# A nine-matmul group of one image of a pair, moved on TensorE from ahead of the mixing to behind the short groups of the second feature

## The chip, the cores and the metric

The kernel runs on one core of one Trainium2 chip. The metric is device time in microseconds (us). A core has a matmul engine (TensorE, PE in the rows, with its weight loads as PEld), a vector engine (VectorE, DVE), an activation engine (ScalarE, ACT), GpSimd (POOL) and a queue that issues transfers (SyncE, SPq). Each engine runs its own instructions in the order written; between engines only semaphores set an order. SBUF is the memory that the engines read, PSUM the one that TensorE writes its sums to.

## The reference, cut to what matters

The input is x of 16 images, 32 channels, 32 by 32 pixels. The first block is dense: each convolution sees x and all the features before it.

```
x1 = relu(conv2d(x, w1, b1, 2, 2))                      # 3x3, padding 2, dilation 2
x2 = relu(conv2d(concat(x, x1), w2, b2, 2, 2))
x3 = relu(conv2d(concat(x, x1, x2), w3, b3, 2, 2))
x4 = relu(conv2d(concat(x, x1, x2, x3), w4, b4, 2, 2))
fea = relu(concat(x, x1, x2, x3, x4))                   # 160 channels
fea = einsum('ij,bcjk,lk->bcil', H, fea, H)             # a 32-point transform on rows and columns
out = conv2d(fea, w6, b6, 1, 1) + x
```

The second block takes `out` through three convolutions with inputs and weights rounded to 4 bits (1x1 to 192 planes, 3x3 by plane, 1x1 back to 32) and adds its input. The change doesn't touch it.

## The kernel before

Images go through the dense block in eight pairs. `step(s, ...)` works on pair s; u is 0 or 1, the image in the pair. There are nine steps: 0, 1 and 2 are written out, 3 to 6 run in a loop of two bodies, 7 and 8 are written out. Step s computes the features of pair s (the convolutions) and, in between, mixes and transforms the pair before, p = s - 1. Step 8 only finishes pair 7.

**Convolutions.** A feature is held in `D[f][u]` as four shifted copies of 32 channels on 128 partitions, in a high and a low half of the float32 value, so that one product takes three matmuls (high by high, high by low, low by high). With three column shifts a full group is 9 matmuls of 128x512 (`conv`, L654 to L662). The 128 output rows of a group hold two features' sums at once. On x itself (f = 0) there are two groups per image: the first (weights 0) gives features 1 and 2 and goes to bank 0 of `conv_ps[u]`, the second (weights 1) gives features 3 and 4 and opens bank 1. Both stand in `conv0` (L682). On feature 1 there are the short groups, six matmuls (`conv1_alone`, L706, with L698 into `conv_ps` and L702 into `mix_ps`), and a full group into bank 1 (`conv1`, L712). On feature 2 there is one full group (`conv2`, L716), on feature 3 again short groups (`conv3`, L721).

**From a sum to the next feature.** ACT takes the sum from PSUM (`relu` L287 and L278, `take_part` L295), DVE adds the parts (`add_parts`, L417 and L419) and splits the feature into its halves (`split`, L406 and L408), the queue copies the shifted partitions (`halos`, L205 and L207), and PE waits for these copies on `halo_in`.

**Mixing.** `mix(p, u)` (L752) makes eight products of three matmuls from `F_hl` (L745) and one from `X4` (L749) in the four banks of `mix_ps`; ACT takes each to `Y` (`take_mix`, L330). `stage1` (L770) transforms one direction out of `Y`, again into `mix_ps`, at the end of a step. DVE turns that result into `Zt` (`turn_s1`, L450), once for each image, and it does so in the step after, right behind the split of feature 1 of image 0. `stage3` (L779) transforms the other direction, DVE turns it back (L457) and adds it up (L473).

**What sets the order around the change.** The order is written by hand for each engine. In a step PE runs `conv0` of both images, `mix(p, 0)`, `conv1_alone` of both, `conv1` of both, `stage3` of both, `conv2` of both, `mix(p, 1)`, `conv3` of both, `stage1`. `mix_ready` (L725) makes the mixing wait on `f_lo` and on `zt_done`: since `mix(p, 0)` overwrites the banks that `stage1` wrote, both transposes L450 of the step must have ended first. `zt_done` starts at GRANT, so in steps 0 and 1 nothing waits on it; in step 1 PE waits for `scales_ready` instead, behind `spread_weights` (L675), which DVE gives in L524 after the split of image 1. ACT holds a loop-like order too: at the end of a step `high_4` and `copy_4` of both images (L313, L320), and then `relu(s, 1, 0)` of the next step. The group that the change moves signals `x_used[1]`, on which ACT's `high_x` of the next pair waits.

Of the kernel before, what the change touches and what calls it, by code (L numbers as in the profile page):

```python
# [70 lines left out]
def dense_block(nc, x_res, x_pads, x_mix, w_conv, bias, w_mix, h_cols, h_rows, b6, w_int, ident_in, keep):  # L71
# [7 lines left out]
    with ExitStack() as ctx:  # L79
# [88 lines left out]
        def is_first(s):  # L168
            return isinstance(s, int) and s == 0

        def has_finish(s):

            return not (isinstance(s, int) and s < 2)

        def is_second(s):
            return isinstance(s, int) and s == 1

        def is_last(s):
            return isinstance(s, int) and s == PAIRS
# [470 lines left out]
        def _(pe):  # L650
# [3 lines left out]
            def conv(u, f, n, bank, start):  # L654

                for d in range(3):
                    for h, (wp, xp) in enumerate(((0, 0), (0, 1), (1, 0))):
                        last = nc.tensor.matmul(conv_ps[u][:, bank, :], w_hl[:, wp, n, d, :],  # L658
                                                D[f][u][:, xp, :, 2 * d:2 * d + S],
                                                start=start and d == 0 and h == 0,  # L660
                                                stop=d == 2 and h == 2, skip_group_check=True)
                return last  # L662

            def weights(s, n):
                if is_first(s):
                    pe.wait_ge(w_ready, n)
# [11 lines left out]
            def transform_ready():  # L678
                pe.wait_ge(h_in, 32)
                pe.wait_ge(w_ready, NM + 2)  # L680

            def conv0(s, u):  # L682
                pe.wait_ge(x_split[u], s + 1)
                if not is_first(s):
                    pe.wait_ge(added[u], s * 2)
                weights(s, 1)
                conv(u, 0, 0, 0, True).then_inc(conv_done[u], 1)
                weights(s, 2)
                conv(u, 0, 1, 1, True).then_inc(x_used[u], 1)

            def conv_alone(s, u, f, n):

                weights(s, n + 1)
                bank, side = conv_ps[u][:, (f - 1) // 2, :], side_sums(u, f)
                for d in range(3):
                    last = nc.tensor.matmul(bank, w_hl[:, 0, n, d, :], D[f - 1][u][:, 1, :, 2 * d:2 * d + S],  # L698
                                            start=False, stop=d == 2, skip_group_check=True)
                last.then_inc(conv_done[u], 1)  # L700
                for d in range(3):
                    last = nc.tensor.matmul(side, w_hl[:, 1, n, d, :], D[f - 1][u][:, 0, :, 2 * d:2 * d + S],  # L702
                                            start=d == 0, stop=d == 2, skip_group_check=True)
                last.then_inc(conv_done[u], 1)

            def conv1_alone(s, u):  # L706
                pe.wait_ge(halo_in[1][u], (s + 1) * 32)
                if not is_first(s):
                    pe.wait_ge(y_out, (s - 1) * 16 + (5 + u))
                conv_alone(s, u, 2, 2)  # L710

            def conv1(s, u):  # L712
                weights(s, 4)
                conv(u, 1, 3, 1, False)
# [10 lines left out]
            def mix_ready(p, u):  # L725

                pe.wait_ge(f_lo[u], p + 1)
                if banks(p, u) is not sums_ps:
                    for done in (zt_done, st_done) if u else (zt_done,):
                        pe.wait_ge(done, p * 2 + GRANT)  # L730

            def mix_x4_ready(p, u):
                pe.wait_ge(x4_lo[u], p + 1)
                pe.wait_ge(x4_copied[u], p + 1)

            def mix_rows(p, u, g):

                h, k = g // 4, slice(NP * (g % 4), NP * (g % 4) + NP)
                if g >= 4:
                    pe.wait_ge(y_out, (p * 2 + u) * 8 + (g - 3))  # L740
                elif banks(p, u) is sums_ps and g % 2 == 0:
                    pe.wait_ge(added[g // 2], 2 * PAIRS)
                y = banks(p, u)[:, g % 4, 0:MIX]
                for n, (wp, xp) in enumerate(((0, 0), (0, 1), (1, 0))):
                    nc.tensor.matmul(y, F_hl[u][:, xp, h, k], mix_hl[:, wp],  # L745
                                     start=n == 0, stop=False, skip_group_check=True)

            def mix_x4(p, u, g):
                nc.tensor.matmul(banks(p, u)[:, g % 4, 0:MIX], X4[u][:, g // 4, NP * (g % 4):NP * (g % 4) + NP],  # L749
                                 mix4_hl[:], start=False, stop=True, skip_group_check=True).then_inc(y_done, 1)  # L750
# [8 lines left out]
            def stage1(p, *us):  # L759

                pe.wait_ge(y_out, p * 16 + 8 * (us[-1] + 1))
                pe.sem_inc(s1_begun, 1)
                out = banks(p, us[0])
                for d in range(3):
                    for j in range(4):
                        k = slice(32 * j, 32 * j + 32)
                        for dy in range(3):
                            at = 96 * d + 32 * dy
                            y = Y[k, us[0]:us[-1] + 1, :, at:at + 32].rearrange("k u g o -> k (u g) o")
                            last = nc.tensor.matmul(out[32 * dy:32 * dy + 32, j, 0:PX // 4 * len(us)], hc[k, d], y,  # L770
                                                    start=d == 0, stop=d == 2, skip_group_check=True)
                last.then_inc(s1_done, 1)

            def stage3(p, u):

                pe.wait_ge(zt_done, p * 2 + (u + 1 + GRANT))
                zt = Zt[:, u, :].rearrange("p (o q l) -> p q o l", q=4, o=C)
                for q in range(4):
                    last = nc.tensor.matmul(banks(p, u)[32 * q:32 * q + 32, 2 + u, 0:PX // 4], hr[:], zt[:, q],  # L779
                                            start=True, stop=True, skip_group_check=True)  # L780
                last.then_inc(s3_done, 1)

            def step(s, odd, batch):
                p = s - 1
                dct = not is_first(s)
                if is_last(s):
                    mix_ready(p, 0)
                    for g in range(4):
                        mix_rows(p, 0, g)
                    mix_x4_ready(p, 0)  # L790
                    for g in range(4):
                        mix_x4(p, 0, g)
                    for g in range(4, 8):
                        mix_rows(p, 0, g)
                        mix_x4(p, 0, g)
                    pe.wait_ge(zt_done, p * 2 + GRANT)
                    for u in range(2):
                        stage3(p - 1, u)
                    mix_ready(p, 1)
                    for g in range(4):  # L800
                        mix_rows(p, 1, g)
                    mix_x4_ready(p, 1)
                    for g in range(4):
                        mix_x4(p, 1, g)
                    stage1(p, 0)
                    for g in range(4, 8):
                        mix_rows(p, 1, g)
                        mix_x4(p, 1, g)
                    stage3(p, 0)
                    stage1(p, 1)  # L810
                    stage3(p, 1)
                    return
                conv0(s, 0)
                conv0(s, 1)
                if is_second(s):
                    transform_ready()
                    spread_weights()
                    pe.wait_ge(scales_ready, 1)
                if dct:
                    mix(p, 0)  # L820
                conv1_alone(s, 0)
                conv1_alone(s, 1)
                conv1(s, 0)
                conv1(s, 1)
                if has_finish(s):
                    pe.wait_ge(y_out, p * 16 + 8)
                    stage3(p - 1, 0)
                    stage3(p - 1, 1)
                conv2(s, 0)
                conv2(s, 1)  # L830
                if is_first(s):
                    turn_peaks()
                if dct:
                    mix(p, 1)
                conv3(s, 0)
                conv3(s, 1)
                if dct:
                    stage1(p, 0, 1)

            steps(pe, step)  # L840


# [481 lines left out]
```

## Time and profile before

| | us |
|---|---|
| median of 3 runs | 429.36 |
| lowest, highest | 428.33, 430.48 |
| the profiled execution's own time | 426.66 |
| span of the profiled execution, first to last instruction | 424.9 |
| PE busy | 371.5 (87% of the span) |
| DVE busy | 299.0 (70%) |
| ACT busy | 232.0 (55%) |
| mean granted clock of TensorE | 0.956 of full speed |

In rows of the timeline the columns are start in us, duration in us, engine, line, operation, output<-inputs, shape and type, the count of instructions merged in the row, and in brackets the idle time before it with what ended that time. Matmuls overlap in the pipeline, so that a row's end lies a little behind the start of the next. The dense block ends at 328 us of the span; the quantised block takes the rest.

### The profile page before, as it was taken

How to read it: one execution, taken by the hardware profiler on the slowest of the kernel's cores; microseconds unless marked ns; L12 is line 12 of the kernel's file. 1: busy time of each engine (PE TensorE's matmuls, PEld its weight loads, DVE VectorE, ACT ScalarE, POOL GpSimd, SP SyncE). 2: the span in 40 equal slices, each digit the busy share in tenths (PEclk: the TensorE clock that was granted, in tenths of full speed). 3: DMA queues.
4: the chain of work that ended last, by engine and by line, in shares of the span. 5: the costliest groups of instructions: out<-in, count | busy, mean ns of one | idle time of the engine just before them, and what ended most of it. 6: DMA issues, size and time to landing. Idle time of an engine off the chain costs nothing. (4 is left out here: it accounts for less than half of the span.)

```text
span 424.9 us, 7855 instructions
## 1 busy us (share of the span) xinstructions
PE 371.5 (87%) x2772; PEld 262.9 (62%) x2772; DVE 299.0 (70%) x552; ACT 232.0 (55%) x378; POOL 18.1 (4%) x18
## 2 busy tenths in 40 slices
PE   4785898999999999999999999999984573799596
PEld 3563686677868778786877878687662221455332
DVE  5546635965884796588479568845976899577866
ACT  5133643655575375457537546752755695177640
POOL 3000000000000000000000000000001700022000
PEclk9998899999999999999999999999998599699969
DMA  7555124532423353242335324034200000000004
GB/s 246 124 146 155 46 53 101 141 76 66 117 77 80 91 151 84 63 108 80 79 92 147 86 64 107 23 77 105 68 3 0 2 0 0 0 4 2 2 26 173
DMA packets 19533, 32.56 MB, mean 77 GB/s; under 512 B 4528, under 2 KB 11568, under 8 KB 19504
## 3 DMA queue, kind: packets, MB, share of 16 engines
q1 hardware_dynamic: 19504, 32.17, 28.9%
q8 instruction: 18, 0.29, 0.3%
q14 instruction: 11, 0.09, 0.1%
HBM read 11.38 MB, written 2.10 MB: 32 GB/s over the span
## 5 line engine op out<-in xcount | busy, mean ns | idle before, releaser
L658 PE MATMUL sums_ps<-D,w_hl 128*128 128x512 f32 x576 | 148.1, 414 | 14.1 <-DVE D L424 6.0
L658 PEld LDWEIGHTS sums_ps<-D,w_hl 128*128 128x128 f32 x576 | 109.8, 193 | 53.5 <-DMA D<-D 8.7
L330 ACT ACTIVATE Y<-mix_ps 128x288 f32<-128x288 f32 x120 | 49.0, 411 | 32.9 <-PE mix_ps L749 20.9
L745 PE MATMUL mix_ps<-mix_hl,F_hl 128*128 128x288 f32 x360 | 65.1, 298 | 1.5 <-DVE St L457 0.7
L745 PEld LDWEIGHTS mix_ps<-mix_hl,F_hl 128*128 128x128 f32 x360 | 55.0, 190 | 5.0 <-issue 2.6
L287 ACT ACTIVATE r<-sums_ps,bias_sb 64x512 f32<-64x512 f32 x32 | 21.9, 683 | 66.2 <-PE sums_ps L658 66.1
L417 DVE TENSOR_TENSOR r<-mix_ps,r 64x512 f32<-64x512 f32 x16 | 11.1, 694 | 43.5 <-PE mix_ps L702 22.0
L406 DVE CAST D<-r 64x512 fp32r<-64x512 f32 x48 | 19.8, 412 | 25.5 <-ACT r L287 25.5
L1151 PE MATMUL ps<-q_q,q_diag 64*64 64x512 bf16 x576 | 34.7, 400 | 2.0 <-DVE q_q L1043 2.0
L955 ACT ACTIVATE q_I<-ps,w_bias 128x1024 f32 x24 | 25.4, 1111 | 18.9 <-PE ps L1151 18.9
L749 PE MATMUL mix_ps<-mix_hl,X 96*128 96x288 f32 x120 | 35.3, 298 | 0.0
L408 DVE TENSOR_TENSOR D<-r,D 64x512 fp32r<-64x512 f32 x48 | 32.9, 685 | 1.7
L698 PE MATMUL sums_ps<-D,w_hl 128*128 128x512 f32 x96 | 29.7, 420 | 4.1 <-DMA D<-D 4.1
L1151 PEld LDWEIGHTS ps<-q_q,q_diag 64*64 64x64 bf16 x576 | 19.3, 108 | 17.0 <-issue 3.8
L295 ACT ACTIVATE r<-sums_ps,bias_sb 64x512 f32<-64x512 f32 x32 | 21.1, 682 | 14.4 <-PE sums_ps L698 14.2
L440 DVE SCALAR_TENSOR_TENSOR X<-r,X 32x512 fp32r<-32x512 f32 x32 | 21.8, 681 | 8.1 <-ACT X L313 7.6
L313 ACT ACTIVATE X<-r 32x512 fp32r<-32x512 f32 x32 | 20.2, 630 | 12.9 <-DVE r L419 12.5
L1130 PE MATMUL ps<-q_xq,w_q 128*128 128x386 bf16 x72 | 17.1, 372 | 9.1 <-DVE q_xq L1008 5.2
L770 PE MATMUL mix_ps<-Y,hc 32*32 32x512 f32 (+1 forms) x576 | 24.3, 567 | 0.0
L698 PEld LDWEIGHTS sums_ps<-D,w_hl 128*128 128x128 f32 x96 | 17.4, 193 | 9.1 <-DMA D<-D 5.9
L473 DVE SCALAR_TENSOR_TENSOR values<-St,b_sb,xb 64x128 f32<-64x128 f32 (+1 forms) x64 | 22.2, 346 | 0.9
L431 DVE SCALAR_TENSOR_TENSOR F_hl<-F,F_hl 128x1024 fp32r<-128x1024 f32 x16 | 19.5, 1224 | 4.4 <-ACT F_hl L304 3.7
(121 smaller groups left out, 437.6 us busy)
## 6 DMA issues: line engine op xcount, KB each, us to landing
D<-D SPq DMA_DIRECT2D x96, 126.0 KB, 2.4
F<-r SPq DMA_DIRECT2D x96, 64.0 KB, 2.0
x_own<-in_x_pads SPq DMA_DIRECT2D x16, 288.0 KB, 3.7
F<-in_x_mix SPq DMA_DIRECT2D x16, 128.0 KB, 2.5
xb<-in_x_res SPq DMA_DIRECT2D x8, 256.0 KB, 2.7
out<-q_res SPq DMA_DIRECT2D x8, 256.0 KB, 2.0
w_raw<-in_w_conv SPq DMA_DIRECT2D x6, 192.0 KB, 3.9
w_raw<-in_w_int SPq DMA_DIRECT2D x1, 843.0 KB, 4.6
```

Source lines behind the costliest of these rows:

```text
L287: nc.scalar.activation(r[u][:].rearrange("p a b l -> p (a b l)"), conv_ps[u][0:64, bank, :], ACT.Relu, bias=bias_sb[0:64, f - 1:f]).then_i ...
L330: nc.scalar.activation(Y[:, u, g], banks(p, u)[:, g % 4, 0:MIX], ACT.Copy).then_inc(y_out, 1)
L408: nc.vector.tensor_tensor(out=D[f][u][0:64, 1, :, 2:2 + S], in0=src, in1=D[f][u][0:64, 0, :, 2:2 + S].bitcast(F32), op=ALU.subtract).then_ ...
L440: last = nc.vector.scalar_tensor_tensor(out=X4[u][low, h], in0=r[u][k].rearrange("p a b l -> p (a b l)"), scalar=0.0, in1=X4[u][k, h].bitc ...
L473: last = nc.vector.scalar_tensor_tensor(out=keep.values[64 * pi:64 * pi + 64, batch, m, PH // 2 * a:PH // 2 * (a + 1), :], in0=st[k, pi], ...
L658: last = nc.tensor.matmul(conv_ps[u][:, bank, :], w_hl[:, wp, n, d, :], D[f][u][:, xp, :, 2 * d:2 * d + S], start=start and d == 0 and h == 0,
L698: last = nc.tensor.matmul(bank, w_hl[:, 0, n, d, :], D[f - 1][u][:, 1, :, 2 * d:2 * d + S], start=False, stop=d == 2, skip_group_check=True)
L745: nc.tensor.matmul(y, F_hl[u][:, xp, h, k], mix_hl[:, wp], start=n == 0, stop=False, skip_group_check=True)
L749: nc.tensor.matmul(banks(p, u)[:, g % 4, 0:MIX], X4[u][:, g // 4, NP * (g % 4):NP * (g % 4) + NP], mix4_hl[:], start=False, stop=True, ski ...
L770: last = nc.tensor.matmul(out[32 * dy:32 * dy + 32, j, 0:PX // 4 * len(us)], hc[k, d], y, start=d == 0, stop=d == 2, skip_group_check=True)
L955: nc.scalar.activation(I[:, g, b, 0:PX], ps[:, 2 * b:2 * b + 2].rearrange("p k n -> p (k n)"), ACT.Relu, bias=keep.w2_bias[:, bass.ts(g, 1 ...
L1151: last = nc.tensor.matmul(ps[64 * col:64 * col + 64, 2 * (two + b) + h], diag[rows, par, at:at + 2].rearrange("p q c -> p (q c)"), field[: ...
```

## The change

`conv0(s, u)` is cut in two. It keeps the first group on x; the second group becomes `conv0_later(s, u)`. For image 0 that still follows at once. For image 1 it now stands behind `conv1_alone(s, 1)`, ahead of `conv1(s, 0)`. The change touches no other engine's order.

```diff
                 conv(u, 0, 0, 0, True).then_inc(conv_done[u], 1)
+
+            def conv0_later(s, u):
                 weights(s, 2)
                 conv(u, 0, 1, 1, True).then_inc(x_used[u], 1)
@@
                 conv0(s, 0)
+                conv0_later(s, 0)
                 conv0(s, 1)
                 if is_second(s):
                     transform_ready()
@@
                 conv1_alone(s, 0)
                 conv1_alone(s, 1)
+                conv0_later(s, 1)
                 conv1(s, 0)
                 conv1(s, 1)
```

The first place is on PE, at the border between step 1 and step 2: the last short groups of `conv3`, `stage1` (L770; L772 with the change), the groups on x (L658) and the start of the mixing (L745, L749; L747, L751 with the change). Before:

```order
L698 MATMUL sums_ps<-D,w_hl 128x512 x3
L702 MATMUL sums_ps<-D,w_hl 128x512 x3
L770 MATMUL mix_ps<-Y,hc 32x512 x36
L658 MATMUL sums_ps<-D,w_hl 128x512 x36
L745 MATMUL mix_ps<-mix_hl,F_hl 128x288 x3
L749 MATMUL mix_ps<-mix_hl,X 128x288
```

The same place with the change:

```order
L700 MATMUL sums_ps<-D,w_hl 128x512 x3
L704 MATMUL sums_ps<-D,w_hl 128x512 x3
L772 MATMUL mix_ps<-Y,hc 32x512 x36
L658 MATMUL sums_ps<-D,w_hl 128x512 x27
L747 MATMUL mix_ps<-mix_hl,F_hl 128x288 x3
L751 MATMUL mix_ps<-mix_hl,X 128x288
```

Between `stage1` and the mixing stand 27 matmuls in place of 36. The second place is on PE later in step 2: the last product of the mixing, the short groups on feature 1 (L698 and L702; L700 and L704 with the change), the full groups, `stage3` (L779; L781 with the change) and `conv2`. Before:

```order
L745 MATMUL mix_ps<-mix_hl,F_hl 128x288 x3
L749 MATMUL mix_ps<-mix_hl,X 128x288
L698 MATMUL sums_ps<-D,w_hl 128x512 x3
L702 MATMUL mix_ps<-D,w_hl 128x512 x3
L698 MATMUL sums_ps<-D,w_hl 128x512 x3
L702 MATMUL mix_ps<-D,w_hl 128x512 x3
L658 MATMUL sums_ps<-D,w_hl 128x512 x18
L779 MATMUL mix_ps<-Zt,hr 32x256 x8
L658 MATMUL sums_ps<-D,w_hl 128x512 x18
```

The same place with the change:

```order
L747 MATMUL mix_ps<-mix_hl,F_hl 128x288 x3
L751 MATMUL mix_ps<-mix_hl,X 128x288
L700 MATMUL sums_ps<-D,w_hl 128x512 x3
L704 MATMUL mix_ps<-D,w_hl 128x512 x3
L700 MATMUL sums_ps<-D,w_hl 128x512 x3
L704 MATMUL mix_ps<-D,w_hl 128x512 x3
L658 MATMUL sums_ps<-D,w_hl 128x512 x27
L781 MATMUL mix_ps<-Zt,hr 32x256 x8
L658 MATMUL sums_ps<-D,w_hl 128x512 x18
```

The nine matmuls now stand ahead of the full groups on feature 1 and of `stage3`.

## Rows read from the trace of the kernel before

**Rows 1.** Windows by step: stretch, length, busy (count) by engine, PE clock, DMA, GB/s; step 4

```profile
157.60:194.70 37.10, 36.63 (x250) 28.22 (x248) 26.41 (x46) 21.30 (x39) 0.00 (x0) 1.00 0.37 94
```

**Rows 2.** Timeline of PE, step 4 and the start of step 5

```profile
157.63 8.99 PE L658 MATMUL sums_ps<-D,w_hl 128*128 128x512 f32 x36
...
166.54 0.67 PE L745 MATMUL mix_ps<-mix_hl,F_hl 128*128 128x288 f32 x3
...
173.86 4.53 PE L658 MATMUL sums_ps<-D,w_hl 128*128 128x512 f32 x18
178.32 1.07 PE L779 MATMUL mix_ps<-Zt,hr 96*32 96x256 f32 x16
179.86 4.65 PE L658 MATMUL sums_ps<-D,w_hl 128*128 128x512 f32 x18 [0.47 <-DMA D<-D]
...
194.78 8.99 PE L658 MATMUL sums_ps<-D,w_hl 128*128 128x512 f32 x36
```

**Rows 3.** Waits of steps 2 to 7, 83 to 306 us: total, times, longest

```profile
PE sums_ps L658 <- DMA D<-D: 2.3, 6, 0.5
...
PEld mix_ps L745 <- DVE Zt L450: 1.2, 4, 0.4
```

**Rows 4.** Timeline of ACT, DVE and PEld up to the mixing of step 4

```profile
161.05 1.27 ACT L320 ACTIVATE X<-r 32x512 fp32r<-32x512 f32 x2
...
163.06 0.42 DVE L406 CAST D<-r 64x512 fp32r<-64x512 f32 x1 [0.63 <-ACT r L287]
...
164.12 2.37 DVE L450 STREAM_TRANSPOSE Zt<-mix_ps 96x1024 f32<-96x1024 f32 x2
...
166.54 0.43 PEld L745 LDWEIGHTS mix_ps<-mix_hl,F_hl 128*128 128x128 f32 x3 [0.36 <-DVE Zt L450]
```

**Rows 5.** Timeline of ACT and DVE, end of step 4

```profile
184.55 0.69 ACT L287 ACTIVATE r<-sums_ps,bias_sb 64x512 f32<-64x512 f32 x1 [1.36 <-PE sums_ps L658]
...
190.22 2.56 DVE L431 SCALAR_TENSOR_TENSOR F_hl<-F,F_hl 128x1024 fp32r<-128x1024 f32 x2
...
194.25 1.27 ACT L313 ACTIVATE X<-r 32x512 fp32r<-32x512 f32 x2 [1.45 <-DVE r L419]
```

**Rows 6.** Timeline of DVE behind stage3 of step 4

```profile
179.03 0.88 DVE L457 STREAM_TRANSPOSE St<-mix_ps 128x256 f32<-128x256 f32 x2 [1.23 <-PE mix_ps L779]
...
183.22 0.42 DVE L406 CAST D<-r 64x512 fp32r<-64x512 f32 x1 [0.65 <-ACT r L287]
```

**Rows 7.** Timeline of PE and DVE, start of step 2

```profile
83.33 8.98 PE L658 MATMUL sums_ps<-D,w_hl 128*128 128x512 f32 x36 [0.42 <-DVE r L419]
...
90.18 2.37 DVE L450 STREAM_TRANSPOSE Zt<-mix_ps 96x1024 f32<-96x1024 f32 x2
```

**Rows 8.** Timeline of PE, steps 0 and 1

```profile
6.05 10.38 PE L658 MATMUL sums_ps<-D,w_hl 128*128 128x512 f32 x36 [6.05 <-DVE D L424]
17.96 0.99 PE L698 MATMUL sums_ps<-D,w_hl 128*128 128x512 f32 x3 [1.54 <-DMA D<-D]
...
28.55 4.65 PE L658 MATMUL sums_ps<-D,w_hl 128*128 128x512 f32 x18 [1.32 <-DMA D<-D]
...
43.75 10.29 PE L658 MATMUL sums_ps<-D,w_hl 128*128 128x512 f32 x36 [2.73 <-DVE r L419]
...
67.95 4.63 PE L658 MATMUL sums_ps<-D,w_hl 128*128 128x512 f32 x18 [1.30 <-DMA D<-D]
```

**Rows 9.** Timeline of DVE and PE, step 1, where the mixing begins

```profile
53.06 0.68 DVE L408 TENSOR_TENSOR D<-r,D 64x512 fp32r<-64x512 f32 x1
54.38 0.16 DVE L522 TENSOR_SCALAR w_scale<-mix_ps 128x3 f32<-128x3 f32 x1 [0.64 <-PE mix_ps L675]
...
54.81 0.67 PE L745 MATMUL mix_ps<-mix_hl,F_hl 128*128 128x288 f32 x3 [0.46 <-DVE inv L524]
```

**Rows 10.** Windows of PE: stretch, length, busy (count), PE clock, DMA, GB/s

```profile
41.00:41.50 0.50, 0.01 (x1) 1.00 0.98 249
...
43.00:43.50 0.50, 0.00 (x0) 0.89 0.06 16
```

## The prediction

> **What bounds the kernel now.** I read the busy time of the engines by step first, since the change touches the dense block alone. A step of the loop takes 37.1 us, of which PE is busy 36.6, DVE 26.4 and ACT 21.3, at the full granted clock [rows 1]. That reads as a kernel bound by PE, in which the order of PE's work is free as long as no wait opens. The timeline of PE says the same: in step 4 the 36 matmuls on x start at 157.63, the mixing at 166.54, and the only idle time in brackets in the whole step is 0.47 us ahead of `conv2`, released by the transfer of the shifted copies [rows 2]. The list of waits gives the sum over steps 2 to 7: six such waits, 2.3 us in all, 0.38 each [rows 3]. This is what the change can win in these steps, and it does aim there, because work put behind the short groups gives feature 2 more time to come back.
>
> The second line of that list is the one that matters. Four times in six steps the weight load of the first mixing matmul waited for DVE's transpose L450, never long [rows 3]. So I looked at what stands right ahead of the mixing on the other engines. In step 4 ACT copies the last `X4` from 161.05 on (1.27 us). It then gives feature 1 to DVE, which splits it at 163.06 and starts the two transposes at 164.12; they end at 164.12 + 2.37 = 166.49. The load for the mixing starts at 166.54 [rows 4]. PE has hardly waited, but only since its 36 matmuls end in the same tenth of a microsecond. Two paths meet at the mixing: PE's own work on x, and a chain ACT, DVE that ends in the transposes. The chain is not short of PE's path by anything.
>
> Where does this chain begin? I followed it back into the step before. ACT's `relu` of feature 3 of image 1 had waited for PE's `conv2` (184.55, behind 1.36 us idle, released by L658). DVE's split and the sums of the pair before follow it without a gap up to the split of F (190.22, 2.56 us, so to 192.78); the added parts of image 0 release ACT at 194.25, and ACT is then busy with `X4` until `relu` of the next step [rows 5]. So the chain hangs on PE's `conv2` of the step before, and not on the 9 matmuls that are moved.
>
> **The change part by part.** *The price of the moved group.* From 157.63 to 166.54 PE issues 36 matmuls: 8.91 / 36 = 0.2475 us each, 9 x 0.2475 = 2.23 us. The number of matmuls is the same before and after, so only waits can change the time.
>
> *Ahead of the mixing, steps 2 to 7 (added wait).* PE has done its 27 matmuls at 166.54 - 2.23 = 164.31 and reaches the mixing. The transposes can't have ended then: DVE only started them at 164.12, and their release (the split of feature 1 of image 0, the `X4` work of ACT) does not depend on the moved group, since the first group of image 0 still comes first and ACT was busy anyway [rows 4]. I expect the mixing to start where it did and PE to stand idle for 2.2 us. Behind the waiting instruction on PE stands everything: mixing, short groups, `conv1`, `stage3`, `conv2`. In step 2 the 27 matmuls end at 83.33 + 8.91 - 2.23 = 90.0 and the transposes at 90.18 + 2.37 = 92.55: idle 2.5 us there [rows 7].
>
> *Behind the short groups (removed wait).* The short groups start where they did, then 2.23 us are added ahead of `conv1`. The full groups, `stage3` and `conv2` come later by 2.23, and the 0.38 us of waiting for the copies is gone, as that transfer hangs on the short groups, which do not move. Net delay of `conv2`: 2.23 - 0.38 = 1.85 us a step. From `conv2` on all hangs together: PE has no gap up to the mixing of the next step, and the chain of ACT and DVE starts at `conv2`. Nothing there gives the time back. Six steps: 6 x 2.23 - 2.3 = 11.1 us.
>
> *Is something late next?* `stage3` comes 2.23 later and DVE's work behind it too, while the split of feature 3 only comes 1.85 later. DVE turns back at 179.03 and had 0.65 us idle ahead of the split at 183.22 [rows 6]; 0.65 - 0.38 = 0.27 is left, so this costs nothing; without this cover it would be at most 0.38 a step, 2.3 in all. The signal `x_used[1]` comes at about 176.1 in place of 166; ACT asks for it behind the `relu` of feature 2. I cost it at nothing; a tenth or two late would go into the same slack.
>
> *Step 1.* Nothing waits for transposes here, but the mixing waits for the weight scales. DVE has to split image 1 first, until 53.06 + 0.68 = 53.74, then waited 0.64 for PE's L675, and from 54.38 it took 0.43 until the mixing at 54.81 [rows 9]. L675 now comes 2.23 earlier, so DVE can go on at 53.74: the mixing starts 0.64 earlier, at 54.17, not 2.23. PE has done its 27 matmuls at 43.75 + 10.29 - 2.23 = 51.8 and idles 2.4. Behind the short groups 2.23 come in and the wait of 1.30 ahead of `conv2` [rows 8] goes. Step 1: -0.64 + 2.23 - 1.30 = +0.3.
>
> *Step 0.* There is no mixing. PE waited for the copies of feature 1 until 17.96, idle for 1.54; now it is there 2.23 earlier and idles 3.8. The 2.23 come in behind the short groups, where `conv2` waited 1.32 for the copies [rows 8]: +0.9. What the clock does decides the rest. In the trace PE stopped at about 41.0 with the granted clock at 1.00, and it was falling before 43.5 [rows 10]; the 36 matmuls behind that gap of 2.73 took 10.29 in place of 8.99, which is 1.3 us [rows 8, 2]. The gap of 1.54 in step 0 had none of this to show. Between the two ends, no fall (0) and one fall (1.3), the 3.8 us are nearest to the row with the fall, so I take 1.3, and step 0 costs 2.2. The later waits of that step hang on PE's `conv2` and pass it on.
>
> *Sum.* 2.2 + 0.3 + 11.1 = 13.6 us. The profiled execution took 426.66, so 440.3; the median of the runs stands 2.7 us above it, at 429.36, and against that I expect 443.0.
>
> *Two rules weighed.* At the mixing the weight load itself stood waiting until 166.54, with the first matmul [rows 4]. The Trainium skill, in "TensorE: Matmul & The Clock Gate", section "Architectural detail: the array is 16× 32×32, not 1× 128×128", says that PE's queue can pull weight loads ahead of matmuls in flight. By that rule the load of 0.14 us would be hidden in the new gap and six steps would cost 0.9 us less; by the row it is held by the same semaphore, and the sum keeps it.
>
> **The rivals.**
>
> *A. The clock falls in the new gaps too.* Place: the mixing of steps 1 to 7, seven gaps of 2.2 to 2.5 us. For it: the fall ahead of 43.5 came 2.4 us after PE had stopped [rows 10]. Against: the gaps of 1.30 to 1.54 had no fall, and most of the new ones are shorter than the gap that had one [rows 8]. Price by the row: 1.3 each, 7 x 1.3 = 9.1, which gives 452; with two or three falls 446 to 447. The same page of the Trainium skill, section "🎯 Why this matters for your kernels", warns against idle gaps between bursts of matmuls, since they bring the array back to half rate; it speaks against this change in just this way.
>
> *B. Faster.* The mixing starts 2.23 earlier, as the order on PE has it, because the transposes are done in time. Then no gap opens, and the waits ahead of `conv2` go: 2.3 in six steps and 1.3 in step 1, less 0.9 in step 0, so -2.7, about 426.7. For it: the list charges only 1.2 us of PE's loads to L450 [rows 3]. Against: the end of the transposes at 166.49. It decides from the point where they end by 164.3, and they would have to start before 162, when ACT has not given feature 1 yet [rows 4].
>
> *C. The chain loosens.* DVE is idle for over 10 us of a step [rows 1]. If the chain to the next transposes followed DVE's own order and not PE's `conv2`, half of the delay could be taken up in each step: 13.6 / 2 = 6.8, so about 436. Against: the idle time of 1.36 released by PE [rows 5].
>
> *D. No difference*, since the two effects cancel: 429. It would need a gap of 0.38 only, and no row shows that.
>
> **How the numbers follow.** Forecast 0.74, own range 440.5 to 446 (step 0 from 0.9 to 3, DVE's slack used up or not, one or two falls, runs that differ by a microsecond). A 0.10, B 0.05, C 0.08, D 0.03. A measurement of this kernel tells apart about 0.5%, 2.1 us. Faster 0.05 (B), same 0.03 (D), slower 0.92. The range is 439.5 to 449.5: it leaves out B, C and D below (0.16) and the upper part of A.
>
> **What would show it.** Right: in each of steps 2 to 7 an idle time of 2.1 to 2.5 us ahead of the first mixing matmul, released by L450; no idle time ahead of `conv2`; steps of about 38.9 us with PE's busy time unchanged; step 1 with a gap of about 2.4 released by L524. In step 0 an idle time of 3.8 ahead of the short groups. Wrong: a mixing that starts within half a microsecond of the 27th matmul (B), steps under 38 us (C), or a granted clock below 1.00 behind the gaps of the loop (A).

## The result, and the profile after

The changed kernel takes 445.20 us (median of 4 runs, 444.02 to 448.65), against 428.85 for the kernel before on the same chips (4 runs, 427.07 to 430.48): ratio 1.0395, interval [1.0323, 1.0468]. The forecast was 443.0 in a range of 439.5 to 449.5, slower with a chance of 0.92. The profiled execution took 444.02 us, its span 442.2 in place of 424.9.

The timeline of PE in step 4, with the columns as before, answers to [rows 2]. Lines behind L690 are two higher in the changed file: the mixing is L747, `stage3` L781.

```profile
163.90 6.81 PE L658 MATMUL sums_ps<-D,w_hl 128*128 128x512 f32 x27
172.78 0.67 PE L747 MATMUL mix_ps<-mix_hl,F_hl 128*128 128x288 f32 x3 [2.07 <-DVE Zt L450]
...
181.59 6.73 PE L658 MATMUL sums_ps<-D,w_hl 128*128 128x512 f32 x27
188.25 1.07 PE L781 MATMUL mix_ps<-Zt,hr 96*32 96x256 f32 x16
189.25 4.62 PE L658 MATMUL sums_ps<-D,w_hl 128*128 128x512 f32 x18
```

The gap ahead of the mixing is there, released by the transpose L450, and the wait ahead of `conv2` is gone: the 18 matmuls at 189.25 have no bracket. From the start of the groups on x to the mixing it is 8.88 us, as before (8.91). PE did less in this stretch and reached the mixing no sooner.

DVE's timeline shows the path that holds the mixing, the answer to [rows 4]: the split of feature 1, and the transposes right behind it, until 170.36 + 2.37 = 172.73.

```profile
169.30 0.42 DVE L406 CAST D<-r 64x512 fp32r<-64x512 f32 x1 [0.63 <-ACT r L287]
...
170.36 2.37 DVE L450 STREAM_TRANSPOSE Zt<-mix_ps 96x1024 f32<-96x1024 f32 x2
```

PE's waits of steps 2 to 7 (84 to 323 us), in total, times and longest, answer to [rows 3]. The two put down to "issue" (the profile shows no releaser) are the same gap, in steps 2 and 7: 2.52 and 2.04 us.

```profile
PE mix_ps L747 <- DVE Zt L450: 8.1, 4, 2.1
PE mix_ps L747 <- issue: 4.6, 2, 2.5
PE sums_ps L658 <- DVE r L419: 0.4, 1, 0.4
```

The windows by step, from the start of the groups on x to the next, answer to [rows 1]: stretch, length, busy time of PE, PEld, DVE, ACT and POOL, the granted clock, the DMA share and GB/s.

```profile
84.61:125.26 40.65, 38.13 (x249) 29.70 (x249) 26.87 (x46) 21.81 (x39) 0.00 (x0) 0.96 0.34 86
125.26:163.90 38.64, 36.68 (x251) 28.23 (x249) 26.27 (x46) 21.17 (x39) 0.00 (x0) 1.00 0.36 91
163.90:204.14 40.24, 38.17 (x250) 29.73 (x248) 26.41 (x46) 21.31 (x39) 0.00 (x0) 0.96 0.36 87
204.14:244.35 40.21, 38.18 (x250) 29.73 (x249) 26.38 (x46) 21.27 (x39) 0.00 (x0) 0.96 0.34 86
244.35:283.10 38.75, 36.70 (x251) 28.22 (x249) 26.45 (x46) 21.35 (x39) 0.00 (x0) 1.00 0.31 74
283.10:323.30 40.20, 38.16 (x250) 29.72 (x248) 25.04 (x44) 20.16 (x37) 0.00 (x0) 0.96 0.29 69
```

Two kinds of step stand here. Two have the full clock and take 38.64 and 38.75 us. Four have a clock of 0.96 and 1.5 us more of PE's busy time, and take 40.2 and more. In step 4 the lower clock lies in the mixing behind the gap (windows of PE alone):

```profile
171.00:172.00 1.00, 0.00 (x0) 1.00 0.50 120
...
173.00:174.00 1.00, 1.00 (x7) 0.68 0.74 182
174.00:177.00 3.00, 3.00 (x15) 0.54 0.49 115
177.00:178.00 1.00, 1.00 (x10) 1.00 0.00 0
```

That is the lower of the clock's two levels, 1.2 GHz in place of 2.4, for 3 to 4 us. The first two steps answer to [rows 8] and [rows 9]:

```profile
17.45 1.65 PE L700 MATMUL sums_ps<-D,w_hl 128*128 128x512 f32 x3 [3.16 <-DMA D<-D]
...
44.95 6.80 PE L658 MATMUL sums_ps<-D,w_hl 128*128 128x512 f32 x27 [3.14 <-DVE r L419]
...
53.98 1.09 PE L747 MATMUL mix_ps<-mix_hl,F_hl 128*128 128x288 f32 x3 [1.92 <-DVE inv L524]
```

In two windows of PE alone the clock of step 1 stands at 1.00 all through the gap of 3.14 us, and at half in the mixing, behind the gap of 1.92:

```profile
42.00:44.50 2.50, 0.00 (x0) 1.00 0.78 257
54.00:57.00 3.00, 3.00 (x12) 0.50 0.67 161
```

Step 1 begins 44.95 - 43.75 = 1.2 us later than before, step 2 84.61 - 83.33 = 1.3. So steps 0 and 1 together cost 1.3, and the six steps behind them 238.7 - 222.4 = 16.3 (they took 83.33 to 305.74 before).

### The profile page after: what moved, and what is told of

It reads as the page before. It is cut to its first block and busy times, and to the rows that moved or that the text cites. A ratio compares the mean times of both kernels' runs of the same rounds, so it can differ in the third digit from the quotient of the medians.

```text
span 442.2 us, 7853 instructions
## 1 busy us (share of the span) xinstructions
PE 379.2 (86%) x2770; PEld 271.8 (61%) x2772; DVE 298.8 (68%) x552; ACT 232.0 (52%) x378; POOL 18.0 (4%) x18
## 5 line engine op out<-in xcount | busy, mean ns | idle before, releaser
L658 PE MATMUL sums_ps<-D,w_hl 128*128 128x512 f32 x576 | 146.5, 412 | 9.4 <-DVE D L424 5.9
L658 PEld LDWEIGHTS sums_ps<-D,w_hl 128*128 128x128 f32 x576 | 109.3, 192 | 47.5 <-issue 8.2
L747 PE MATMUL mix_ps<-mix_hl,F_hl 128*128 128x288 f32 x360 | 72.0, 319 | 15.3 <-DVE Zt L450 8.1
L747 PEld LDWEIGHTS mix_ps<-mix_hl,F_hl 128*128 128x128 f32 x360 | 61.2, 211 | 19.5 <-DVE Zt L450 9.9
L417 DVE TENSOR_TENSOR r<-mix_ps,r 64x512 f32<-64x512 f32 x16 | 11.1, 693 | 51.5 <-PE mix_ps L704 27.0
L751 PE MATMUL mix_ps<-mix_hl,X 96*128 96x288 f32 x120 | 37.9, 320 | 0.0
L700 PE MATMUL sums_ps<-D,w_hl 128*128 128x512 f32 x96 | 31.0, 435 | 4.3 <-DMA D<-D 4.3
L751 PEld LDWEIGHTS mix_ps<-mix_hl,X 96*128 96x128 f32 x120 | 24.9, 209 | 0.0
L772 PE MATMUL mix_ps<-Y,hc 32*32 32x512 f32 (+1 forms) x576 | 24.3, 567 | 0.0
L700 PEld LDWEIGHTS sums_ps<-D,w_hl 128*128 128x128 f32 x96 | 18.2, 203 | 9.5 <-DMA D<-D 6.2
```

The lines of the kernel that those rows point to most:

```text
L747: nc.tensor.matmul(y, F_hl[u][:, xp, h, k], mix_hl[:, wp], start=n == 0, stop=False, skip_group_check=True)
```

## The experiments

Each kernel was timed against runs of the kernel before on its own chip; that kernel's medians there were 427.5 to 427.9.

**e1: fill the gap with useless work.** The moved group is also run in its old place; the second run overwrites it.

```diff
+            def filler(s, u):
+                if has_finish(s):
+                    conv(u, 0, 1, 1, True)
...
                 conv0(s, 1)
+                filler(s, 1)
```

> The changed kernel, with the nine moved matmuls also run once more in their old place in steps 2 to 7 (the second run in the new place overwrites the result, so this is pure extra work of 6 x 2.23 us on PE that fills the idle time ahead of the mixing). Theory (the mixing is held by the transposes L450; on top of that the clock falls in some of the idle gaps): PE does the extra work in the gap for nothing, the granted clock stays at 1.00 in steps 2 to 7, each of these steps takes 38.6 to 38.8 us (as the two steps of the changed kernel without a fall), and the kernel takes 438 to 439 us, about 6 us less than the changed one although it does more. Rival (the clock in the loop has no part, the 6 us beyond the waits come from longer mixings for another reason): 444 to 446. Rival (PE is bound by its own work): 13.4 us more than the changed kernel, 458.

Measured: 440.01 us (439.11 to 441.72), ratio 1.0297 [1.0250, 1.0345], with 54 matmuls more than the changed kernel. That one stood 16.4 us above the kernel before on its chips, this one 12.1 on its own: about 4 us less. Its PE timeline (mixing at L751) and a window over nearly all of the six steps (85.76 to 318.55):

```profile
163.58 9.01 PE L658 MATMUL sums_ps<-D,w_hl 128*128 128x512 f32 x36
172.48 0.67 PE L751 MATMUL mix_ps<-mix_hl,F_hl 128*128 128x288 f32 x3
```

```profile
84.00:315.00 231.00, 230.26 (x1505) 178.61 (x1488) 155.66 (x268) 125.03 (x224) 0.00 (x0) 1.00 0.35 85
```

From 163.58 to the mixing it is 8.90 us again, now without a gap; the clock stays at 1.00, and steps 3 to 7 take 38.7 to 38.8 (step 2: 39.16). Two things are shown: the place ahead of the mixing is free for 2.2 us of PE's work, since DVE's path takes as long, and the falls of the clock come from the gap. The total came 1 us above what I expected. In its profile step 2 starts at 85.76 in place of 84.61: with the order of the changed kernel in steps 0 and 1, its 27 matmuls at the start of step 1 took 8.28 us in place of 6.80.

**e5: move three matmuls in place of nine.** One column shift of the group (0.74 us) goes behind the short groups.

```diff
-                conv(u, 0, 1, 1, True).then_inc(x_used[u], 1)
+                if u == 0:
+                    conv(u, 0, 1, 1, True).then_inc(x_used[u], 1)
+                else:
+                    conv(u, 0, 1, 1, True, (0, 1))
+            def conv0_rest(u):
+                conv(u, 0, 1, 1, True, (2,)).then_inc(x_used[u], 1)
...
                 conv1_alone(s, 1)
+                conv0_rest(1)
```

> The kernel before with only the last three of the nine matmuls (one column shift, 0.74 us) moved behind the short groups. Theory: a gap of 0.6 to 0.7 us ahead of the mixing, too short for a fall, and the wait of 0.38 ahead of conv2 gone: +0.25 a step in six steps, 1.5 in all; step 0 has room (0), step 1 wins about 0.6. Ratio 1.001 to 1.004. Rival (each moved matmul costs the same share of the 16 us): +5.4 us, ratio 1.013. Rival (moving work there helps as long as it is short): ratio below 0.997.

Measured: 427.91 us (427.30 to 429.60), ratio 1.0000 [0.9977, 1.0024]. PE in step 4 (mixing at L751):

```profile
157.67 8.31 PE L658 MATMUL sums_ps<-D,w_hl 128*128 128x512 f32 x33
166.54 0.66 PE L751 MATMUL mix_ps<-mix_hl,F_hl 128*128 128x288 f32 x3 [0.57 <-DVE Zt L450]
...
180.01 4.62 PE L658 MATMUL sums_ps<-D,w_hl 128*128 128x512 f32 x18
```

The mixing starts 8.87 us behind the start of the step, where it was 8.91 before [rows 2]. The gap is 0.57, the wait ahead of `conv2` is gone, and steps 3 to 7 take 37.1 to 37.2 in place of 37.0 to 37.1 (step 2: 37.65 in place of 37.31, with a gap of 1.02). The six steps are 1.25 us longer in its profile, where I expected 1.5. The total can't be told from the kernel before nor from the 1.001 that the forecast began with; the rival at 1.013 is out. The cost does not grow in proportion: three of nine matmuls cost about a tenth of the loss of a step. Up to some 0.4 us the removed wait pays for the gap, and none of these gaps had a fall of the clock.

**e2 and e3: take the transposes off the path.** DVE does both at the end of the step before, where it mostly waits for ACT; e2 does this to the kernel before, e3 to the changed one.

```diff
                 split(s, 1, 0)
-                if has_finish(s):
-                    turn_s1(p - 1, 0)
-                    turn_s1(p - 1, 1)
                 split(s, 1, 1)
...
                 low_4(s, 0)
-                if is_before_last(s):
+                if not is_first(s):
                     turn_s1(p, 0)
                 low_4(s, 1)
+                if not is_first(s) and not is_before_last(s):
+                    turn_s1(p, 1)
```

> The kernel before with one edit on DVE: the two transposes L450 that a step did behind the split of feature 1 are done at the end of the step before, one between low_4 of image 0 and of image 1, one behind low_4 of image 1. Theory: they end about 2.7 us ahead of the mixing then, but with the old order PE was hardly held by them, so the time moves by less than 1 us: steps of 36.9 to 37.1, ratio 0.997 to 1.001. Rival (the transposes were the true bound of a step): steps fall below 36.8, ratio under 0.995. Rival (low_4 and the split come late for it): ratio over 1.003.

Measured: 427.38 us (424.99 to 429.11), ratio 0.9982 [0.9954, 1.0010]: no difference that can be told, as expected. Its steps take 36.74 to 36.95.

> The changed kernel with the same edit on DVE (transposes at the end of the step before). Theory: the loss of the change hangs on the transposes alone. With them early the mixing starts behind the 27th matmul, no gap, no fall of the clock in steps 2 to 7, and the wait ahead of conv2 is gone as well: steps of 36.6 to 36.7, 2.4 us won in six steps, 1.3 us lost in steps 0 and 1, so 427.5, ratio to the kernel before 0.995 to 0.999. Rival (the later conv1, stage3 and conv2 delay the chain whatever the mixing does): steps of 38.6, ratio 1.023 or more.

Measured: 435.29 us (433.14 to 436.19), ratio 1.0164 [1.0125, 1.0204]. Neither side was right. In steps 2 to 7 the gap and the falls are gone, and over half of the loss with them (16.4 us to 7.4, each against the kernel before on its own chips), but steps 3 to 7 take 37.7 and not 36.6 (step 2: 38.19). PE in step 4, where the short groups are L699 and L703:

```profile
161.79 6.82 PE L657 MATMUL sums_ps<-D,w_hl 128*128 128x512 f32 x27
...
173.46 0.89 PE L703 MATMUL mix_ps<-D,w_hl 128*128 128x512 f32 x3
175.41 0.99 PE L699 MATMUL sums_ps<-D,w_hl 128*128 128x512 f32 x3 [1.06 <-DMA D<-D]
```

```profile
PE sums_ps L699 <- DMA D<-D: 6.5, 6, 1.4
```

With the mixing on time, PE is at the short groups of image 1 before the shifted copies of that image's feature 1 have landed: six waits, 6.5 us. With the old waits ahead of `conv2` gone (2.3 us) that makes 4.2, and the six steps are 4.4 us longer than before (226.8 against 222.4). Steps 0 and 1, which have the order of the changed kernel, are 2.5 us longer in this profile. The nine matmuls had covered that transfer too, behind the transposes, where it could not be seen.

Part of this wait stands in the queue. DVE has split feature 1 of image 1 at 169.81 + 0.68 = 170.49, and the queue issues the copies only from 172.24 on, behind the other transfers of its order:

```profile
171.00 1.19 SPq L220 DMA_DIRECT2D F<-r  x2
172.24 0.63 SPq L205 DMA_DIRECT2D D<-D  x1
172.91 0.61 SPq L207 DMA_DIRECT2D D<-D  x1
```

The second transpose also does not fit wholly into idle time in its new place. It ends at 166.62 + 1.23 = 167.85, and the split of feature 1 of image 0 starts at 167.88, though ACT had given that feature at 167.17: 0.7 us late. No run moves the transposes or the transfers elsewhere to tell the two shares apart.

**e4: only one transpose early.** As e3, with the second transpose left behind the split.

```diff
                 if has_finish(s):
-                    turn_s1(p - 1, 0)
                     turn_s1(p - 1, 1)
...
-                if is_before_last(s):
+                if not is_first(s):
                     turn_s1(p, 0)
```

> The changed kernel with only the first of the two transposes L450 done at the end of the step before. Theory (the idle time ahead of the mixing is as long as DVE's path through the transposes makes it): 1.23 us of transposing leaves the path, so the gap falls from 2.05 to about 0.8, too short for a fall of the clock; steps of 37.4 to 37.7 in place of 38.7 and 40.2; total 433 to 435, near e3. Rival (only the second transpose's place or the split counts): steps stay at 38.6 and more, 440 to 445.

Measured: 434.60 us (433.29 to 435.27), ratio 1.0166 [1.0115, 1.0217]. The gap follows DVE's path: 0.96 in place of 2.07, so 1.1 less for a transpose of 1.23, released by the same line (0.85 to 0.96 in steps 3 to 7, 1.38 in step 2), and no fall of the clock in steps 2 to 7. Steps 3 to 7 take 37.5 to 37.7, and the total lies in the expected range.

```profile
168.77 0.66 PE L746 MATMUL mix_ps<-mix_hl,F_hl 128*128 128x288 f32 x3 [0.96 <-DVE Zt L450]
```

**e7: another place behind the mixing.** In steps 2 to 7 the nine matmuls stand between the two images' short groups; the transposes are late, steps 0 and 1 as before.

```diff
                 conv0(s, 1)
+                if not has_finish(s):
+                    conv0_later(s, 1)
...
                 conv1_alone(s, 0)
+                if has_finish(s):
+                    conv0_later(s, 1)
                 conv1_alone(s, 1)
```

> As e6 but with the transposes where they were (behind the split of feature 1), so the nine matmuls stand between the two images' short groups in steps 2 to 7, steps 0 and 1 as before. Theory: the gap ahead of the mixing (2.05 us) and its falls of the clock are those of the changed kernel, since all that counts is that the group has left the place ahead of the mixing: steps of 38.65 without and 40.2 with a fall, 442 to 445, about 1 us under the changed kernel for steps 0 and 1. Rival (its place behind the short groups of both images is what costs): steps of 37.1, 428 to 430.

Measured: 446.74 us (445.70 to 448.34), ratio 1.0448 [1.0394, 1.0503]. The gap is the same, 2.10 in step 4, and four of the six steps have a fall, so the rival is out. The total lies 1.7 us above the expected range. What I missed by 0.4 us a step (39.07 in step 5, without a fall) is for the most part the second row: `conv2` waits as in the kernel before, six times, 1.8 us.

```profile
173.13 0.66 PE L747 MATMUL mix_ps<-mix_hl,F_hl 128*128 128x288 f32 x3 [2.10 <-DVE Zt L450]
...
190.00 4.64 PE L658 MATMUL sums_ps<-D,w_hl 128*128 128x512 f32 x18 [0.34 <-DMA D<-D]
```

**e8: the change from step 2 on.** Both calls of `conv0_later(s, 1)` as in e7, the second behind the short groups of image 1.

> The change in steps 2 to 7 only; steps 0 and 1 have the order of the kernel before. Theory: the first two steps cost 1.3 us net in the changed kernel (0.9 for the group that comes in behind the short groups, the rest for falls of the clock gained and lost), so this kernel takes 1 to 2 us less than the changed one, 443 to 444. Rival (the fall in step 0 is a cost of its own of 1.3 and more): 441 or less.

Measured: 444.93 us (443.11 to 447.13), ratio 1.0412 [1.0355, 1.0470]. The runs can't tell it from the changed kernel. In its profile step 2 begins at 83.71 in place of 84.61, so the first two steps give back 0.9. The six steps behind them are as long as in the changed kernel (238.8 and 238.7), with four falls in both. The rest of the span, which the change does not touch, took 120.6 us here and 118.9 there, which hides the 0.9; over all the profiles it took 118.9 to 121.3. What the fall in step 0 costs by itself stays open.

**e6: cover both transfers.** e3's transposes and e7's place. The diff is the sum of those two.

> Both transposes early, as in e3, and in steps 2 to 7 the nine matmuls stand between the short groups of image 0 and those of image 1 (steps 0 and 1 as in the kernel before). Theory (in e3 a second wait took the place of the first: the copies of feature 1 of image 1, 0.9 to 1.4 us a step ahead of the short groups of image 1, for want of the moved 2.23 us ahead of them): here the moved group covers that transfer and still stands behind the group that starts feature 2, so neither wait is left. PE without a gap: steps of 36.6 to 36.7 in place of 37.0 to 37.1, 2.2 us less than the kernel before, ratio 0.993 to 0.997. Rival (the transfer of feature 1 of image 0 is late as well once the mixing starts 2.2 us earlier): steps of 37.0 or more, ratio 1.000 or more.

Measured: 426.71 us (425.40 to 427.48), ratio 0.9979 [0.9956, 1.0002]; run again on another chip as e10:

> e6 once more, timed on the same chip as e9, to tell whether it is faster than the kernel before. Theory: steps of 36.75 in place of 37.0 to 37.1, 1.5 to 2 us under the kernel before, ratio 0.995 to 0.998. Rival (e6 only drew a good chip): ratio 0.999 to 1.002.

426.84 us (425.09 to 428.97), ratio 0.9991 [0.9970, 1.0011]. Neither timing tells it apart from the kernel before, and both ratios lie above the range that I expected. In the profiles of e6 and e10 the six steps take 220.8 and 221.0 us, against 222.4 before and 221.3 in e2, with most steps at 36.75 to 36.8 and not 36.6 to 36.7. PE in step 4, and the waits of its steps 2 to 7:

```profile
157.47 6.82 PE L657 MATMUL sums_ps<-D,w_hl 128*128 128x512 f32 x27
168.41 0.89 PE L699 MATMUL sums_ps<-D,w_hl 128*128 128x512 f32 x3
...
172.05 0.89 PE L699 MATMUL sums_ps<-D,w_hl 128*128 128x512 f32 x3
...
179.35 4.65 PE L657 MATMUL sums_ps<-D,w_hl 128*128 128x512 f32 x18 [0.31 <-DMA D<-D]
```

```profile
PE sums_ps L657 <- DMA D<-D: 1.8, 6, 0.3
```

No wait ahead of the mixing or of either short group; only the old one ahead of `conv2` is left. On ACT, `relu` of feature 2 of image 0 stands behind the `take_part` of image 1, and that waits for image 1's short groups, which have come later:

```profile
172.98 0.69 ACT L295 ACTIVATE r<-sums_ps,bias_sb 64x512 f32<-64x512 f32 x1 [2.79 <-PE sums_ps L699]
173.69 0.63 ACT L278 ACTIVATE r<-r 64x512 f32<-64x512 f32 x1
```

**e9: finish image 0 first.** e6, with ACT and DVE working image by image on feature 2.

```diff
                 take_part(s, 2, 0)
+                if has_finish(s):
+                    relu(s, 2, 0)
+                    take_part(s, 2, 1)
...
                 add_parts(s, 2, 0)
+                if has_finish(s):
+                    split(s, 2, 0)
+                    add_parts(s, 2, 1)
```

> As e6, and in steps 2 to 7 ACT and DVE finish feature 2 of image 0 before they turn to image 1 (ACT: relu of image 0 ahead of take_part of image 1; DVE: split of image 0 ahead of add_parts of image 1). Theory (the 0.3 us that conv2 still waits in e6 come from ACT's order: relu of image 0 stands behind the take_part of image 1, which waits for that image's short groups): the copies of image 0 come about 2 us earlier, the wait ahead of conv2 goes, steps of 36.4 to 36.5, 1.8 us under e6, 425.0, ratio to the kernel before 0.992 to 0.996. Rival (the transfers in the queue are what is late): the wait of 0.3 stays, ratio 0.997 to 1.000.

Measured: 424.74 us (423.63 to 426.50), ratio 0.9943 [0.9920, 0.9966]: faster than the kernel before by about half a percent, as expected, and 2.1 us under e6 on the same chip. PE in step 4 (`conv2` is L665 there, `stage3` L788), and a window over five of the six steps:

```profile
178.75 1.07 PE L788 MATMUL mix_ps<-Zt,hr 96*32 96x256 f32 x16
179.75 4.84 PE L665 MATMUL sums_ps<-D,w_hl 128*128 128x512 f32 x18
```

```profile
117.00:306.00 189.00, 189.00 (x1331) 145.35 (x1329) 138.37 (x232) 109.64 (x196) 0.00 (x0) 1.00 0.36 90
```

PE is busy in all of the 189 us, the wait ahead of `conv2` is gone, and the steps take 36.4 to 36.6. The three edits together (the group behind image 0's short groups, the transposes early, feature 2 image by image) are worth 2.8 us. What the group's new place is worth in this is not shown: no run has the two other edits with the group in its old place, and with the transposes alone early (e2) the six steps are already about half a us from e6's.

## Why the prediction was right, and where its sizes were off

**The mechanism.** The step that carried the forecast, that the mixing would start where it did because the transposes hold it, is shown from four sides: the gap's releaser and its length in the changed kernel; e1, in which 2.2 us of extra work fit in it; e5, in which the mixing stays 8.87 us behind the start of the step; and e4, in which the gap shrinks by nearly a transpose. That the delay of `conv2` is passed on and not made up is shown by the two steps at full clock: 38.64 and 38.75, where [rows 1] gave 37.1.

**The price of a step.** Forecast 1.85, measured 1.65 at full clock. One row that the sum used was a little short: the 0.47 of [rows 2] counts from the end of a matmul's tail, while PE now starts `conv2` 0.07 before that end (188.25 + 1.07 = 189.32, start 189.25). So the removed wait was worth 0.54 there, not 0.47. The rest, 0.13 a step, is in part in three stretches of step 4 that came out 0.03 shorter each: 8.88 for 8.91 up to the mixing, 6.66 - 4.46 = 2.20 for the 2.23 of the nine matmuls, 14.89 for 14.92 from `conv2` to the next step. Six steps: 9.9 where I had 11.1.

**DVE's cover.** The slack of 0.65 was forecast to shrink to 0.27 and shrank to almost nothing: in the changed kernel `add_up` ends at 192.49 and the split of feature 3 starts at 192.59 without idle time. It cost nothing that a step's length shows.

**Steps 0 and 1.** Forecast 2.2 and 0.3, measured 1.2 and 0.1. In step 0 the idle time was there (3.16 us, where I had 3.8 from the matmuls' starts and a start-up that itself ran differently), and the clock fell, as forecast. But the fall that the kernel before had at the start of step 1 ([rows 8]: 10.29 us) did not come this time, and a fall came in the mixing of step 1 instead. So the 0.1 of step 1 holds a fall of 1.3 us that did not come and one of 1.5 that came. They nearly cancel, which the sum did not foresee. Falls move about between runs: in e1 and e4, with the changed kernel's order in steps 0 and 1, the 27 matmuls at the start of step 1 took 8.28 and 8.25 us, where the row above has 6.80. There the mixing starts 10.51 and 10.47 us behind the start of step 1, in place of 11.06, close to the 0.64 less that I had forecast. The gap ahead of it is 1.92 and not 2.4.

**The clock in the loop.** This is the term that was mis-sized. I had priced falls in the gaps of the loop at nothing in the sum and given them a chance of 0.10 as rival A. Four of six gaps of 2.0 to 2.5 us had one, at 40.2 - 38.7 = 1.5 us each, 6 in all. By my own test (a clock below 1.00 behind the gaps) rival A was right in mechanism and in part in size. Between the two profiles the loss is 444.02 - 426.66 = 17.4 us, where the sum had 13.6: the falls that it left out are worth 6, and its other terms were too large by 2.4 (13.6 against 1.3 + 9.9). That the forecast landed within 2.2 us of the median is thus in part luck, two errors of opposite sign. The one row on which I had put the bound, a fall that came 2.4 us after PE had stopped, showed one such time and not the shortest. The Trainium skill ("TensorE: Matmul & The Clock Gate", section "🎯 Why this matters for your kernels") warns against idle gaps between bursts. The gaps that it means are longer than the ones here, so it did not speak against this change in the way that I had written; it had the sign of this term all the same, and on the size the measurement decides. e1 shows the term, with the clock back at 1.00 and about 4 us less for more work.

**The other rule.** The first weight load of the mixing was not pulled into the gap: it stands at 172.78 with the first matmul, and the mixing starts 0.05 us behind the end of the transposes (172.73, 172.78), as before.

**The rivals.** B (no gap) fell with the gap. But B also held that without the gap the change would win 2.7 us, and e3 shows that this is wrong as well: with the transposes out of the way the six steps still take 4.4 us more than before, by a transfer that no row of the kernel before showed as a wait, and steps 0 and 1 cost 2.5 more. C fell with the steps' length, D with the result.

## What to carry to other kernels

Work that stands ahead of a wait which a profile shows as short or absent may be just what makes it short. Before moving it, read when each thing that the next instruction needs is ready, not only the one that came last: here there were two behind one another, a transpose and a transfer. With both covered anew the loss of the move was gone (e6), but a gain by the move alone is not shown. Where PE would stand idle for 2 us in every round of a loop, count the clock as well: in e1 useless work in the gap was cheaper than the gap.

## What the runs showed of the hardware that was not expected

Gaps of 2.0 to 2.1 us between stretches of dense matmuls were enough for a fall of TensorE's clock in three of five cases in the changed kernel, in four of five in e7 and in three of five in e8: ten of fifteen. The gap of 2.5 in step 2 had a fall in two of these three profiles. The gaps of up to 1.4 us in e3 and e4 and of up to 1.0 in e5 had none in steps 2 to 7. The length of a gap alone does not decide: in the changed kernel PE stood idle for 3.14 us ahead of step 1 with the granted clock at 1.00 throughout, and the clock fell behind the next gap, of 1.92. What else decides is not shown. A fall in the mixing cost 1.5 us. The changed kernel's runs spread over 4.6 us (444.02 to 448.65), and the longest has the lowest mean clock (0.927, against 0.934 and 0.935 in the others).
